# Banded attention in a chain of twelve sub-layers on one core: values as stationary weights in two column halves, the softmax division ahead of the transposes, and the sums of the exponentials on VectorE

## The reference, cut to what matters

```python
h = shift_token(x)                       # second half of the channels one token later
q, k, v = split(h @ wqkv)                # 8 heads of 64
q, k = rotary_xpos(l2norm(q) * qs, l2norm(k) * ksc)
sim  = einsum('bhwid,bhwjd->bhwij', q * 8, look_around(k))
sim  = where((i < j) | (i > j + 64) | (j == -1), -max, sim)
attn = softmax(sim)                      # exp(sim - max) / sum
o    = einsum('bhwij,bhwjd->bhwid', attn, look_around(v))
x    = x + o @ wo
```

## Time and profile before

| | us |
|---|---|
| median of 3 runs | 6490.51 (6477.3 to 6496.55) |
| the profiled execution | 6487.8 |
| its span | 6486.0 |
| TensorE busy | 5117.7, 79% of the span |
| VectorE busy | 4383.5, 68% |
| ScalarE busy | 3185.1, 49% |
| GpSimd busy | 2010.0, 31% |

### The profile page before, as it was taken

One profiled execution on the slowest core, in us unless ns is written; L12 is line 12 of the kernel. 1 busy time (PEld: TensorE's weight loads), 2 busy tenths in 40 slices (PEclk: granted clock), 3 DMA queues, 4 the chain that ended last, 5 costly groups with the idle time before them and its releaser, 6 DMA issues. The chain is left out here.

```text
span 6486.0 us, 113128 instructions
## 1 busy us (share of the span) xinstructions
PE 5117.7 (79%) x33035; PEld 3577.2 (55%) x33132; DVE 4383.5 (68%) x10948; ACT 3185.1 (49%) x5879; POOL 2010.0 (31%) x1367
## 2 busy tenths in 40 slices
PE   6777888777779879979979879866678648596777
PEld 5665555466657647636647647634433445343564
DVE  6997777699967647638857647647645268363774
ACT  6776888677755535537745535531111320203223
POOL 6995111199934224212224224200120000200110
PEclk8999999899989999989989989975589755798888
DMA  1000988500000000000000000000100000100000
GB/s 29 0 0 12 303 287 277 178 0 0 0 11 0 4 11 0 0 9 1 1 11 0 3 11 0 3 8 7 33 20 1 1 13 10 43 0 14 0 0 17
DMA packets 162591, 213.91 MB, mean 33 GB/s; under 512 B 54804, under 2 KB 90984, under 8 KB 162408
## 3 DMA queue, kind: packets, MB, share of 16 engines
q1 hardware_dynamic: 160360, 207.73, 10.1%
q0 software_dynamic: 2048, 4.20, 0.3%
HBM read 104.91 MB, written 106.95 MB: 33 GB/s over the span
## 5 line engine op out<-in xcount | busy, mean ns | idle before, releaser
L1836 POOL TENSOR_TENSOR l0b_S<-l0b_sim 128x1024 f32<-128x1024 f32 x256 | 494.0, 1968 | 135.2 <-ACT l0b_sim L1899 115.6
L1836 POOL TENSOR_TENSOR l0a_S<-l0a_sim 128x1024 f32<-128x1024 f32 x256 | 494.2, 1968 | 80.8 <-ACT l0a_sim L1899 63.1
L1969 DVE SCALAR_TENSOR_TENSOR l0a_w<-l0a_S,l0a_best,l0a_SG 128x1024 f32<-128x1024 f32 x256 | 311.2, 1276 | 8.7 <-ACT l0a_SG L1916 4.4
L1969 DVE SCALAR_TENSOR_TENSOR l0b_w<-l0b_S,l0b_best,l0b_SG 128x1024 f32<-128x1024 f32 x256 | 311.1, 1276 | 8.4 <-ACT l0b_SG L1916 4.1
L1871 PE MATMUL l0a_WT<-ident,l0a_w 128*128 128x128 f32 x2048 | 266.8, 285 | 62.4 <-DVE l0a_w L1969 57.3
L1871 PE MATMUL l0b_WT<-ident,l0b_w 128*128 128x128 f32 x2048 | 265.1, 284 | 63.9 <-DVE l0b_w L1969 58.6
L1871 PEld LDWEIGHTS l0a_WT<-ident,l0a_w 128*128 128x128 f32 x2048 | 237.1, 147 | 106.9 <-DVE l0a_w L1969 106.8
L1871 PEld LDWEIGHTS l0b_WT<-ident,l0b_w 128*128 128x128 f32 x2048 | 234.3, 145 | 109.5 <-DVE l0b_w L1969 109.3
L1916 ACT ACTIVATE l0a_SG<-l0a_S 128x1024 f32<-128x1024 f32 x256 | 260.0, 1024 | 52.8 <-DVE l0a_w L1969 47.6
L1916 ACT ACTIVATE l0b_SG<-l0b_S 128x1024 f32<-128x1024 f32 x256 | 260.0, 1024 | 52.6 <-DVE l0b_w L1969 47.3
L2283 ACT ACT_TABLE_LOAD x16 | 20.5, 1283 | 510.1 <-PE l2ae_IO L2266 255.6
(11 more groups left out here) (707 smaller groups left out, 14288.9 us busy)
## 6 DMA issues: line engine op xcount, KB each, us to landing
shifted_rows<-l0att_XS SPq DMA_DIRECT2D x256, 384.0 KB, 3.2
l0att_BD<-shifted_rows SPq DMA_DIRECT2D x256, 256.0 KB, 3.4
enter_raw<-L_attn_w SPq DMA_DIRECT2D x4, 512.0 KB, 7.0
token_rows<-l2ar_rows SPq DMA_DIRECT2D x32, 64.0 KB, 1.5
l2ae_wgt<-L_ffn_gate_w SPq DMA_DIRECT2D x32, 64.0 KB, 2.1
l2ae_wut<-L_ffn_up_w SPq DMA_DIRECT2D x32, 64.0 KB, 2.0
l2ae_wdt<-L_ffn_down_w SPq DMA_DIRECT2D x32, 64.0 KB, 2.0
token_rows<-l2br_rows SPq DMA_DIRECT2D x32, 64.0 KB, 1.5
```

The source lines that it names most:

```text
L1836: pool.tensor_tensor(S[:, h, :].rearrange("p (a c) -> p a c", a=NK), a, c, ALU.add).then_inc(sm["summed"], 1)
L1969: dve.scalar_tensor_tensor(w[:, h % W_RING, :], S[:, h, :], best[:, s, h, 7:8], SG[:, h % SG_RING, :], ALU.is_ge, ALU.mult).then_inc(sm["w ...
```

## The change

V becomes the stationary operand. `attend` writes the result already turned: head 2g into partitions 0 to 63 and head 2g+1 into 64 to 127 of OV, with a 128x64 block of V as weights and 128 columns of ETa or ETb moving. Since queries now lie along the free axis, the division has to come before: VectorE sums the exponentials in SBUF and inverts the sums (a new `invert`), GpSimd multiplies E by them in place (`weigh`), and `turn_unit` waits for that. `turn_out` and `normalize` go, `output` is 4 matmuls of 256 columns in place of 8 of 128, and OV is copied to oT by ScalarE (`keep_first`, queries 0 to 127) and VectorE (`keep_second`). The memset of V goes. `turn_unit` and `attend` of a unit stand one third later: A has those of unit 2 of sequence n-1, B of unit 0, C of unit 1.

```diff
-        V = ph.sb("V", [P, 2, 2, NH, HD + 1])
+        V = ph.sb("V", [P, 2, 2, NH, HD])
...
+                def weigh(n, u):                                   # GpSimd
+                    pool.wait_ge(sm["recips"], 3 * n + u + 1)
...
+                    pool.tensor_tensor(E, E, share, ALU.mult).then_inc(sm["weighed"], 1)
...
                 def sequence(n, par):                              # GpSimd
...
+                    weigh(n, 0)
+                    if not last_one(n):
+                        scale(n + 1, 0)
+                        rotate(n + 1, 1, used(n))
+                    weigh(n, 1)
+                    if not last_one(n):
+                        scale(n + 1, 1)
+                        rotate(n + 2, 0, use(n, 2) + 1)
+                    weigh(n, 2)
...
+                def output(n, par):                                # TensorE
+                    pe.wait_ge(sm["kept0"], n + 1)
+                    pe.wait_ge(sm["kept1"], n + 1)
+                    for g in range(4):
+                        last = pe.matmul(OV[:, 1, 0:L], wo[:, g, :], oT[:, par, g, :], start=g == 0, stop=g == 3)
...
+                def attend(n, par, u, at):
...
+                    if u == 1 and not first(n):
+                        pe.wait_ge(sm["added"], n)
                     for k in range(2):
                         pe.wait_ge(sm[f"copied{k}"], at + 1)
+                    for g in range(4 if u == 0 else 2):
+                        pair = g if u == 0 else 2 * (u - 1) + g
+                        for c in range(1 if u == 0 else 2):
+                            for k in range(2):
+                                ET = (ETa, ETb)[k]
+                                last = pe.matmul(OV[64 * k:64 * k + 64, min(u, 1), pair * P:(pair + 1) * P],
+                                                 V[:, par, c, 2 * pair + k, :], ET[:, g if u == 0 else 2 * g + c, :],
...
                     score(n, 1)                                    # TensorE, third A
-                    turn_unit(n, 0)
+                    if not first(n):
+                        turn_unit(n - 1, 2, use(n, 0))
                     (project)
-                        turn_out(n - 1, use(n, 1))
-                    attend(n, par, 0)
+                        attend(n - 1, 1 - par, 2, use(n, 0))
                     score(n, 2)                                    # B
-                    turn_unit(n, 1)
-                        output(n - 1, use(n, 1))
+                    turn_unit(n, 0, use(n, 1))
                     (turn_qk(n + 1, 0), project)
-                    attend(n, par, 1)
+                    attend(n, par, 0, use(n, 1))
                     score(n + 1, 0)                                # C
-                    turn_unit(n, 2)
+                    turn_unit(n, 1, use(n, 3))
+                        output(n - 1, 1 - par)
                     (values, turn_qk(n + 1, 1))
-                    attend(n, par, 2)
+                    attend(n, par, 1, use(n, 3))
...
+                def invert(n, u):                                  # VectorE
+                    dve.wait_ge(sm["exped"], 3 * n + u + 1)
...
+                    dve.tensor_reduce(total[:, heads], E, AX, ALU.add).then_inc(sm["totalled"], 1)
+                    dve.wait_ge(sm["totalled"], 3 * n + u + 1)
+                    dve.reciprocal(rec[:, heads], total[:, heads]).then_inc(sm["recips"], 1)
...
                     largest(n, 1)                                  # VectorE, A
+                    invert(n, 0)
+                    (copy to ETb, refine(n + 1, 0), multiply(n + 1, 1))
                     largest(n, 2)                                  # B
+                    invert(n, 1)
+                    (copy to ETb), keep_second(n - 1), (sum_squares(n + 1, 1), refine(n + 1, 1), multiply(n + 2, 0))
                     largest(n + 1, 0)                              # C
+                    invert(n, 2)
+                    (copy to ETb, residual(n - 1), sum_squares(n + 2, 0), copy to QKT)
```

More of the change, by code:

```diff
@@ L991, in use, with used @@
         def use(n, k):
[L993 to L995 removed]
+            if last_one(n) and k > 2:
                 k -= 1
[L997 removed]
+            return 1 + 5 * n + k
+        def used(n):
+            return 2 if first(n) else 1 + 5 * n
         def sequences(engine, body):
@@ L1130, in turn_qk @@
                     turn(0, at, [qk[:, t, 1, 2 * g:2 * g + 2, :] for g in range(4)])
[L1132 to L1137, removed]
+                def output(n, par):
[3 more added lines that the diff above has]
+                        last = pe.matmul(OV[:, 1, 0:L], wo[:, g, :], oT[:, par, g, :], start=g == 0, stop=g == 3)
+                    last.then_inc(sm["final"], 1)
@@ L1139, in output @@
+                def attend(n, par, u, at):
+                    pe.wait_ge(sm["v_copied"], n + 1)
+                    if u == 0 and not first(n):
+                        pe.wait_ge(sm["kept0"], n)
+                    if u == 1 and not first(n):
+                        pe.wait_ge(sm["added"], n)
                     for k in range(2):
                         pe.wait_ge(sm[f"copied{k}"], at + 1)
[L1141 to L1161, removed]
+                    for g in range(4 if u == 0 else 2):
[5 more added lines that the diff above has]
+                                                 V[:, par, c, 2 * pair + k, :], ET[:, g if u == 0 else 2 * g + c, :],
+                                                 start=c == 0, stop=u == 0 or c == 1)
@@ L1382, in sequence @@
                     largest(n, 1)
-                    copy(use(n, 0), ETb[:, :, :])
+                    invert(n, 0)
+                    if not first(n):
+                        copy(use(n, 0), ETb[:, :, :])
                     if not last_one(n):
@@ L1386, in sequence @@
                         multiply(n + 1, 1)
+                    largest(n, 2)
+                    invert(n, 1)
+                    copy(use(n, 1), ETb[:, :, :])
                     if not first(n):
-                        copy(use(n, 1), oT[:, :, P:L])
-                    normalize(n, 0)
-                    largest(n, 2)
-                    copy(use(n, 2), ETb[:, :, :])
+                        keep_second(n - 1, 1 - par)
                     if not last_one(n):
                         sum_squares(n + 1, 1)
+                        refine(n + 1, 1)
+                        multiply(n + 2, 0)
+                    if not last_one(n):
+                        largest(n + 1, 0)
+                    invert(n, 2)
+                    copy(use(n, 3), ETb[:, :, :])
                     if not first(n):
@@ L1397, in sequence @@
                     if not last_one(n):
-                        refine(n + 1, 1)
-                        multiply(n + 2, 0)
-                    normalize(n, 1)
-                    if not last_one(n):
-                        largest(n + 1, 0)
-                    copy(use(n, 4), ETb[:, :, :])
-                    if not last_one(n):
                         sum_squares(n + 2, 0)
-                        copy(use(n, 5), queries(1))
-                    normalize(n, 2)
+                        copy(use(n, 4), queries(1))
                 sequences(dve, sequence)
-                copy(use(LAST, 5), oT[:, :, P:L])
+                copy(use(LAST, 4), ETb[:, :, :])
+                keep_second(LAST, LAST % 2)
                 residual(LAST)
```

111 lines of the change are left out of this document (49 added, 62 removed).

## The result

The kernel after takes 6693.95 us (median of 4, 6684.68 to 6698.37), the kernel before beside it 6490.28 (6477.3 to 6496.55). The ratio is 1.0315, interval 1.0295 to 1.0334: slower by 3.1%, some 204 us, where I forecast 6496 and gave 6420 to 6605. The span went from 6486.0 to 6682.9 us.

A forecast was written before the change was run, and what follows sets the result against it. TensorE, gapless before, set the period; its saved time would become waits on VectorE's copy, period 21.76 against 21.71 us. 1.4 us a run, four runs 5.6, gave 6493; with 2.7 for the median, 6496 us, range 6420 to 6605.

The forecast's parts named there:

- TensorE's savings: Transposes of O gone (0.87 us), output 0.07 less, three attends 2.19 less: TensorE's work per sequence from 21.71 to 18.58 us.
- The first rival: In attend, the two column halves don't overlap: 1.73 us an attend, period 23.6, 6602 us; chance 0.10.
- VectorE's and GpSimd's prices: Operation times per sequence: VectorE net +1.7 us, 17.3 to 19.0; GpSimd's weigh 1.90 or 1.43, 4.8 us more.
- The bound of 0.05 us a group: Each VectorE price may be off by 0.05 us over 8 groups: 0.4 us a sequence, 22 us either way.
- The walk round the sequence: Order of waits in one looped sequence: TensorE waits 2.5 us for bank 1 of TU; period 21.76 against 21.71 us.
- Its program runs without a wait: VectorE's row from largest of unit 1 to the ETb copy of unit 0 at 8.08 us, with refine at 0.61.
- They are all covered, by 1 us or more: GpSimd's weigh and scale operations finish before their results are wanted, though weigh adds 4.8 us a sequence.
- The third rival: TensorE's clock falls around the 2.5 us gap and its transposes: 3.3 us a sequence, +185, 6680 us; chance 0.12.
- Ends: First and last sequences of a run: 19.4 us against 20.2, and 21.1 against 19.6; together +0.7 us a run.

The follow-up runs named there:

- e8: Changed kernel with e6's order in A; in B VectorE copies ETb, sums squares, runs keep_second and refine before invert of unit 1: 6470.92 us (0.9965 of the kernel before).
- e6: Changed kernel with VectorE's refine moved ahead of invert of unit 0, GpSimd's order untouched: 6514.75 us (1.0043 of the kernel before).
- e7: Kernel before with one more GpSimd product of 128x1024 a sequence, on unused tiles, beside refine of the second half: 6484.67 us (1.0002).
- e2: Changed kernel with three more 512-column matmuls in TensorE's gap before the transposes of queries and keys: 6568.59 us (1.0127 of the kernel before).
- e4: Changed kernel with the edits of e1 and e3 together: 6631.83 us (1.0218 of the kernel before).
- e1: Changed kernel with GpSimd's scale placed before weigh of unit 0: 6629.77 us (1.0214 of the kernel before).
- e3: Changed kernel with VectorE's copy to ETb placed before invert of unit 1: 6597.38 us (1.0168 of the kernel before).
- e5: Changed kernel with VectorE's copy to ETb, then refine, before invert in A, and the copy before invert in B: 6531.46 us (1.0068 of the kernel before).

## Why the prediction was wrong

**TensorE's savings: right.** The attend's halves run side by side: two records start at the same time, and 16 take 2057.95 - 2056.93 = 1.02 us, with 0.10 ahead of them behind the transposes (I had 1.00, one after the other is 1.72). Output is 1.72 from start to start, as priced. The first rival is refuted.

**VectorE's and GpSimd's prices: right when alone.** Reductions of E 1.21 and 0.94, weigh 1.90 and 1.47, ETb 0.69. The bound of 0.05 us a group held for these. It did not hold for largest, which takes 0.88 and 0.86 us from start to start (2059.35 to 2060.23, 2066.53 to 2067.39) where I had 1.02, nor for refine. VectorE's work of a sequence, 19.0 us as I added it up, is 18.4 in e8.

**The walk round the sequence: right as a walk.** The place that closes the circle (bank 1 of TU, freed by VectorE's copy behind largest and invert) is the one found. Without the two terms below, e6 has 21.90 where the walk had 21.76. That it agrees to 0.14 us is luck in part: the bank comes 0.24 us sooner there (8.68 for 8.92) and the rest takes 0.38 longer (13.22 for 12.84). The gap in e6 is 1.72 us where I had 2.5, and the wait ahead of attend up to 1.0 where I had 0.7.

**The step that failed: "Its program runs without a wait ... refine 0.61", and "They are all covered, by 1 us or more" of GpSimd's weigh.** I asked when weigh's result was wanted, and not whether the operation disturbs what runs beside it. It does: refine took 2.02 us from 2062.18 to 2064.20. The earlier trace rows have no sign of it: in the kernel before, no operation of refine stood beside a GpSimd product. Its trace had one elsewhere, which I passed over: the clip in C of each sequence.

```profile
2012.32 0.39 POOL L1034 COPY l1a_att_xs<-XN 64x256 f32 x1 [1.28 <-PE l1a_att_PJ L1091]
2012.43 0.31 DVE L1317 TENSOR_SCALAR l1a_att_clipped<-l1a_att_ssum 128x16 f32<-128x16 f32 x1
```

The same instruction takes 0.17 us at 2003.57. Here it takes 0.31 and ends at 2012.74, 0.03 us behind a GpSimd copy on other tiles that ends at 2012.71. In the four runs of the function 51 clips took 0.21 to 0.34 us, each of them to 0.03 us behind the end of such a copy.

The Trainium skill had the rule, in "SBUF — State Buffer", section "SBUF: two separate sides": VectorE and GpSimd share a pair of ports under an exclusive lock for the whole of an instruction, and a VectorE operation with two operands in SBUF takes it. The traces agree: 1.50 us in the kernel after, 1.38 in e7, against 0.17. An estimate of the hold needs, beside my own prices, one time from the kernel after: weigh starts about with the copy to ETb (0.2 us behind its start in the kernel after) and takes 1.90, the copy 0.6, the operation itself 0.2, so 0.2 + 1.9 - 0.6 - 0.2 = 1.3 us, 56 x 1.3 = 73, and 6496 + 73 = 6569. e2, with the hold and without the clock, measured 6568.59; that they meet to a microsecond is chance, with three matmuls more in e2 and the runs' ends in neither sum.

**The third rival, "The clock": right in kind.** I gave it 0.12 and 3.3 us a sequence; it came, at 2.0 us (e2), for 4.5 us of the lower clock a sequence where I had 6.5, and the hold had made the gap 3.4 us where the walk had 2.5. It was not a rival beside the forecast but stood behind it: a small lengthening of the gap set it off. Its time, 6680, is near the measured one by chance, since it had the clock too dear and the hold not at all. The rule of the Trainium skill that the prediction names ("TensorE: Matmul & The Clock Gate", Part 4), that transposes don't count as work, is not settled here. In e6 eight transposes, 1.72 us of nothing and eight transposes left the clock at 1.00. Gaps of 2.02 and 0.78 us with transposes between brought it down in 13 of 13 sequences in e4 and in 8 of 13 in e1, and the longer single gap of 2.2 to 2.3 us did in 8 of 13 in e3. That leans towards the rule and does not show it.

**Ends.** I had +0.7 us a run; the trace gives about (204 - 182)/4 = 5.5. The first sequence takes 23.4 us (1886.02 to 1909.41, from its scores of unit 1 to the next) where I had 19.4, and the last 22.9 where I had 21.1. Part of it is the clock and the hold: in the first sequence the third operation of refine takes 1.79 us, at 1890.02, and ends with the weigh. e8, whose loop has neither, still shows some 5 us a run, though the clock is down in its last sequences too (10.2 us of the last 26.7 in the first run). So the term was too small by itself; by how much is not shown.

**The range.** Its upper end, 6605, took the halves as the dearest likely case, and the bounds left out any pair of things that come together. I had the clock at 6680 and 0.12, and left that outside the range.

## What to carry to other kernels

When work goes to GpSimd, list which VectorE operations can stand beside it, and of those the ones that were held here: both operands in SBUF, or the clip, one SBUF operand and a number. Each, however small, may cost what is left of the GpSimd operation. A small operation that takes longer in one place than in another, and ends with a GpSimd operation, is the sign to look for in the kernel before. Put them ahead of what starts GpSimd (here, refine before the reciprocal), and leave reductions, reciprocals and reads of PSUM beside it. And where a change opens a gap on a TensorE that was full, price it twice: a gap of 1.7 us cost only itself, behind gaps of 2.2 to 2.3 us the clock fell in 8 sequences of 13, and behind one of 3.4 us it fell in each and cost 2 us more a sequence.

## What the hardware showed that I had not expected

- A VectorE operation of 16 elements a partition stood 1.2 to 1.3 us for a GpSimd product on other tiles (0.17 free, 1.50 in the kernel after, 1.38 in e7), and ended 0.03 us behind it or less. Its record begins at its usual place, so that it looks like a long operation, and no wait is shown.
- An operation with a number and one operand, SBUF to SBUF, is held too: the clip of 0.17 us took 0.90 in e5 beside a product and 0.31 in the kernel before beside a copy. Not everything from SBUF to SBUF is: the reciprocal of the sums took its 0.18 us beside GpSimd's rotate (at 2068.37, rotate from 2066.79 to 2069.14).
- Beside the same GpSimd products the reductions (1.21 us), the copies from PSUM (0.69) and the product of a PSUM and an SBUF tile (1.22) kept their times. Whether a GpSimd operation that only writes holds VectorE wasn't tried.
- In the kernel after the clock fell 2.3 to 4.0 us after the start of a gap of 3.3 to 3.4 us and stayed down for 3.4 or 6.8 us, in the longer cases through transposes and a whole projection; at a gap of 2.32 us it fell in some sequences and not in others of the same run.
